# Routing weights spread from SBUF instead of DRAM, and the two ends of an expert stage put in another order

## The reference, cut to what matters

```
scores   = sigmoid(x @ gate_w.T)                    # 32 experts
# best 2 of 4 groups, then the best 8 experts of a token;
# their scores, normalised and times 2.5, are its weights, all others are 0
out      = sum over e of weight[t, e] * down_e(silu(gate_e(x)) * up_e(x))   # 32 routed experts
out     += the shared expert of inner width 256     # no weight; done as 2 units of 128
# second layer: attention, then a feed-forward whose weights w1, w2 are rounded to
# integers after division by a scale = max|w| / 127
```

## Time and profile before

| | us |
|---|---|
| median of 3 runs (417.43 to 422.83) | 417.8 |
| the profiled execution, its own time | 418.78 |
| span of its trace | 417.0 |
| PE busy | 386.8 (93%) |
| DVE busy | 258.8 (62%) |
| ACT busy | 187.5 (45%) |
| POOL busy | 131.3 (31%) |

### The profile page before, as it was taken

One profiled execution on the slowest core, in us unless ns is written; L12 is line 12 of the kernel. 1 busy time (PEld: TensorE's weight loads), 2 busy tenths in 40 slices (PEclk: granted clock), 3 DMA queues, 4 the chain that ended last, 5 costly groups with the idle time before them and its releaser, 6 DMA issues.

```text
span 417.0 us, 8560 instructions
## 1 busy us (share of the span) xinstructions
PE 386.8 (93%) x3269; PEld 314.5 (75%) x3269; DVE 258.8 (62%) x525; ACT 187.5 (45%) x401; POOL 131.3 (31%) x109
## 2 busy tenths in 40 slices
PE   8898699998999899999999999999988999999675
PEld 6554478656787687999999999999986755567333
DVE  0258877589876854555555555555564558844686
ACT  0154722348342533444444554444435488634171
POOL 0125300163030052344333334433385047620012
PEclk9999989998999999999999999999999999999798
DMA  8940000300042006254554554444200000000001
GB/s 300 331 173 2 3 3 2 101 0 4 2 163 66 0 9 230 68 137 134 135 145 145 155 142 147 134 134 146 84 0 0 2 0 2 2 3 1 0 2 58
DMA packets 13916, 32.96 MB, mean 79 GB/s; under 512 B 1760, under 2 KB 3744, under 8 KB 13376
## 3 DMA queue, kind: packets, MB, share of 16 engines
q1 hardware_dynamic: 12000, 30.66, 23.4%
q10 hardware_dynamic: 1888, 1.91, 1.3%
HBM read 31.88 MB, written 0.68 MB: 78 GB/s over the span
## 4 chain that ended last, share of the span: by engine, by line
PE 69%; DVE 19%; ACT 5%; issue 4%; DMA 2%; ACTq 1%; POOL 0%; DVEq 0%
PE psum L1087 68%; DVE rc L847 3%; DMA region<-in_w_lin 2%; DVE rn L826 1%; ACT region L725 1%; DVE xn L774 1%; DVE nt L768 1%; DVE rn L825 1%; DVE nt L770 1%; DVE nt L771 1%; DVE region L848 1%; DVE xc L759 1%; DVE ra L816 1%; ACT sq L541 1%; DVE al L985 1%
## 5 line engine op out<-in xcount | busy, mean ns | idle before, releaser
L1087 PE MATMUL psum<-xh,split_all 128*128 128x296 f32 x544 | 122.9, 300 | 1.4 <-DVE rt L927 1.3
L443 POOL TENSOR_TENSOR split_all<-km,split_all 128x768 fp32r<-128x768 f32 x34 | 63.3, 1863 | 115.9 <-ACT split_all L654 115.9
L1087 PEld LDWEIGHTS psum<-xh,split_all 128*128 128x128 f32 x544 | 91.7, 188 | 2.7 <-DVE rt L927 1.8
L1087 PE MATMUL psum<-xl,split_all 128*128 128x296 f32 (+1 forms) x288 | 85.1, 300 | 0.0
L1087 PE MATMUL psum<-ah,split_all 128*128 128x296 f32 x272 | 67.6, 302 | 2.6 <-DVE al L985 2.0
L674 ACT ACTIVATE ah<-rt 128x296 fp32r<-128x296 f32 x68 | 30.7, 452 | 80.6 <-DVE rt L983 74.3
L1087 PEld LDWEIGHTS psum<-xl,split_all 128*128 128x128 f32 (+1 forms) x288 | 53.2, 187 | 3.2 <-issue 2.8
L985 DVE TENSOR_TENSOR al<-rt,ah 128x296 fp32r<-128x296 f32 x64 | 31.9, 498 | 33.1 <-ACT ah L674 33.1
L1087 PEld LDWEIGHTS psum<-ah,split_all 128*128 128x128 f32 x272 | 47.8, 189 | 5.0 <-DVE al L985 2.5
L980 DVE TENSOR_TENSOR rb<-psum,wb 128x296 f32<-128x296 f32 x60 | 28.0, 467 | 26.4 <-ACT psum L672 26.4
L1087 PE MATMUL psum<-al,split_all 128*128 128x296 f32 x136 | 40.8, 300 | 0.0
(11 more groups left out here) (179 smaller groups left out, 579.0 us busy)
## 6 DMA issues: line engine op xcount, KB each, us to landing
km<-in_experts SPq DMA_DIRECT2D x34, 384.0 KB, 4.0
wb<-weights SPq DMA_DIRECT2D x30, 296.0 KB, 3.7
w_sb<-in_w SPq DMA_DIRECT2D x2, 1024.0 KB, 11.9
region<-in_x SPq DMA_DIRECT2D x6, 296.0 KB, 5.5
region<-in_g_wo SPq DMA_DIRECT2D x1, 1024.0 KB, 4.9
region<-in_l_wo SPq DMA_DIRECT2D x1, 1024.0 KB, 5.0
region<-in_w_lin ACTq DMA_DIRECT2D x6, 128.0 KB, 6.7
qkv_sb<-in_qkv_w SPq DMA_DIRECT2D x1, 768.0 KB, 6.0
```

Source lines behind the costliest of these rows:

```text
L443: nc.gpsimd.tensor_tensor(wl[i], ring[i], wh[i].bitcast(f32), ALU.subtract)\
L1087: return nc.tensor.matmul(out_, lhsT, rhs, start=start, stop=stop, skip_group_check=True)
```

## The change

- The scratch tensor in DRAM, its store and the two selections by PE are gone. Each of the 32 routed units gets its row by a DMA whose source is the row's one partition of `wrow`, read once for each of the 128 partitions it is written to. SP's loop is written out.
- Head: all four first high parts are made before the normalisation, and POOL makes the four low parts in one go; the scale of w1 and w2 is worked out before the router; the sigmoid table is loaded before the tokens are rounded; the shared units use banks 4, 5 and 6, 7 in turn.
- `down_sums` issues its four matmuls on `ah` first and waits for `al` only before the last two.
- Tail: w1 and w2 are quantised and region is cleared in small pieces, one behind each low part from unit 4 on.

```
-BUSY = ((7, (0, 4, 14)), (0, (5, 0, 10)), (3, (5, 4, 8)), (7, (6, 4, 14)), (3, (5, 4, 10)))
+BUSY = ((7, (0, 4, 14)), (0, (5, 0, 10)), (3, (5, 0, 8)), (7, (6, 4, 14)), (3, (5, 4, 10)))
+WPIECES, VPIECES = 8, 8
+VZ = 1 + VPIECES + 2
...
-            def spread_weights(i, row):
-                sp.dma_start(wb[:, i, :], row.broadcast_to([P, T])).then_inc(s_wb[i], 16)
+            def spread_weights(u):
+                row = wrow[u - SHARED:u - SHARED + 1, :].unsqueeze(1).broadcast_to([1, P, T])
+                sp.dma_start(wb[:, u % NRING, :], row).then_inc(s_wb[u % NRING], 16)
 
             for u in range(NRING, 2 * NRING):
-                if u == NRING + 2:
-                    sp.wait_ge(s_wrow, 2)
-                    sp.dma_start(weights, wrow[:, 0:T]).then_inc(s_wout, 16)
-                    sp.wait_ge(s_wout, 16)
-                    for i in range(NRING):
-                        spread_weights(i, weights[NRING + i - SHARED:NRING + i - SHARED + 1, :])
                 load_expert(u, experts[u, :, :])
...
+            sp.wait_ge(s_wrow, 2)
+            for u in range(SHARED, NRING + SHARED):
+                spread_weights(u)
+            for u in range(2 * NRING, UNITS + SHARED):
+                if u < UNITS:
+                    load_expert(u, experts[u, :, :])
+                sp.wait_ge(s_act, 2 * (u - SHARED + 1 - NRING))
+                spread_weights(u - SHARED)
...
+            for u in range(NRING, UNITS):
                 low_part(u, u % NRING)
...
+                k = u - NRING
+                if k == 0:
+                    pool.wait_ge(s_sc, 1)
+                    pool.wait_ge(s_wo, 4)
+                if k < 2 * WPIECES:
+                    quantise_piece(k)
+                elif k < 2 * WPIECES + VPIECES:
+                    clear_piece(k - 2 * WPIECES)
...
-            for i in range(AHEAD):
+            for i in range(NRING):
                 high_part(i, i, 0, False)
             norm(2)
+            load_table(ACT.Sigmoid)
...
             centre(2)
+            reduce_peaks(0, 2, 6, 1)
             norm_apply(2, 6)
...
-            reduce_peaks(0, 2, 7, 1)
+            scales_of(0, 2, 7, 1).then_inc(s_sc, 1)
...
             for u in range(SHARED, NRING):
+                dve.wait_ge(s_wb[u], 16)
                 for j in range(2):
-                    dve.wait_ge(s_sel, 2 * (u - SHARED) + j + 1)
-                    expert_unit(2 * u + j, j, sg[:, j, :], ps[6 + j][:, 0:HALF])
+                    expert_unit(2 * u + j, j, ps[6 + j][:, 0:HALF], wb[:, u, half(j)])
...
+                pe.wait_ge(s_ah, n + 1)
+                for m in range(C):
+                    cols = slice(2 * D + m * P, 2 * D + (m + 1) * P)
+                    for w in (wh, wl):
+                        mm(ps[2 * m + hf][:, 0:HALF], w[i][:, cols], ah[:, hf, :], False, False)
                 if shared:
                     pe.wait_ge(s_alp, n + 1)
                 else:
                     pe.wait_ge(s_al, n + (1 - 2 * SHARED))
                 for m in range(C):
                     cols = slice(2 * D + m * P, 2 * D + (m + 1) * P)
-                    ins = three(ps[2 * m + hf][:, 0:HALF], (wh[i][:, cols], wl[i][:, cols]),
-                                (ah[:, hf, :], al[:, hf, :]), False, False)
+                    ins = mm(ps[2 * m + hf][:, 0:HALF], wh[i][:, cols], al[:, hf, :], False, False)
```

More of the change, by code:

```diff
@@ L165, in program @@
         zeros = sb("zeros", [P, HALF], bf16)
[L166 removed]
+        wrow = sb("wrow", [EXPERTS, T])
         xh = sb("xh", [P, C, T], f32r)
@@ L475, in _, with quantise_piece @@
[L475 to L478, removed]
+            for i in range(NRING):
+                low_part(i, i)
+            for n in range(2 * SHARED):
+                activation_low_part(n, n % 2)
+            def quantise_piece(k):
+                w, wq_ = ((w1_sb, w1q), (w2_sb, w2q))[k // WPIECES]
+                cols = slice(k % WPIECES * WPIECE, (k % WPIECES + 1) * WPIECE)
+                nc.gpsimd.tensor_scalar(w[:, cols], w[:, cols], inv[:, k // WPIECES:k // WPIECES + 1], ROUND,
+                                        ALU.mult, ALU.add).then_inc(s_wqt, 1)
+                pool.wait_ge(s_wqt, k + 1)
+                nc.gpsimd.tensor_scalar(wq_[:].rearrange("p c n -> p (c n)")[:, cols], w[:, cols], 1.0, -ROUND,
+                                        ALU.mult, ALU.add).then_inc(s_wq, 1)
@@ new lines, in clear_piece @@
+            def clear_piece(k):
+                cols = slice(k * VPIECE, (k + 1) * VPIECE)
+                nc.gpsimd.memset(region[:, cols], 0.0).then_inc(s_vz, 1)
+            for u in range(NRING, UNITS):
+                low_part(u, u % NRING)
+                k = u - NRING
[6 more added lines that the diff above has]
+                    clear_piece(k - 2 * WPIECES)
+                elif k == 2 * WPIECES + VPIECES:
+                    pool.wait_ge(s_vz, 1 + VPIECES)
+                    pool.wait_ge(s_wsl, u + 1)
+                    for b in range(2):
+                        nc.gpsimd.memset(v16[64 * b:64 * b + S, :, :, b, HD:HD + 1], 1.0).then_inc(s_vz, 1)
+                    pool.wait_ge(s_vz, VZ)
@@ L667, in _, with expert_unit @@
             load_table(ACT.Silu)
-            def expert_unit(n, j, gate):
+            def expert_unit(n, j, gate, bank=4):
                 act_e.wait_ge(s_g, n + 1)
-                nc.scalar.activation(gate, ps[4][:, 0:HALF], ACT.Silu).then_inc(s_sg, 1)
+                nc.scalar.activation(gate, ps[bank][:, 0:HALF], ACT.Silu).then_inc(s_sg, 1)
                 act_e.wait_ge(s_act, n + 1)
                 nc.scalar.activation(ah[:, j, :], act[:, j, :], ACT.Copy).then_inc(s_ah, 1)
[L676 to L679, removed]
+            for i in range(SHARED):
+                for j in range(2):
+                    expert_unit(2 * i + j, j, sg[:, j, :], 4 + 2 * j)
+            for i in range(SHARED, NRING):
+                if i == SHARED:
+                    act_e.wait_ge(s_wrow, 2)
+                expert_unit(2 * i, 0, ps[6][:, 0:HALF])
+                high_part(i + AHEAD, (i + AHEAD) % NRING, (i + AHEAD) // NRING)
+                expert_unit(2 * i + 1, 1, ps[7][:, 0:HALF])
             with act_e.Fori(1, (UNITS - AHEAD) // NRING) as r:
@@ L1369, in three, with up_sums @@
                 return mm(out_, w_lo, x_hi, False, stop)
-            def up_sums(u, i, hf, first=False):
-                n = 2 * u + hf
+            def up_sums(u, i, hf, bank=4, waits=None):
+                n = 2 * u + hf if waits is None else waits
                 if hf == 0:
                     pe.wait_ge(s_wsl, u + 1)
-                if not first:
+                if waits != 0:
                     pe.wait_ge(s_sg, n)
@@ L1379, in up_sums @@
                     cols = slice(c * INNER, (c + 1) * INNER)
-                    ins = three(ps[4][:, 0:HALF], (wh[i][:, cols], wl[i][:, cols]),
+                    ins = three(ps[bank][:, 0:HALF], (wh[i][:, cols], wl[i][:, cols]),
                                 (xh[:, c, half(hf)], xl[:, c, half(hf)]), c == 0, c == C - 1)
                 ins.then_inc(s_g, 1)
-                if not first:
+                if waits != 0:
                     pe.wait_ge(s_act, n)
@@ L1642 @@
     out = nc.dram_tensor("out", (P, C, T), mybir.dt.float32, kind="ExternalOutput").ap()
-    weights = nc.dram_tensor("weights", (EXPERTS, T), mybir.dt.float32, kind="Internal").ap()
-    program(nc, *args, weights, out)
+    program(nc, *args, out)
     r = run_bass_kernel_spmd(nc, [{f"in_{k}": arrays[k] for k in _ORDER}], core_ids=[0])
```

91 lines of the change are left out of this document (24 added, 67 removed).

## The result

| | before | changed |
|---|---|---|
| median | 417.62 (416.55 to 422.83, 4 runs) | **605.52** (605.06 to 607.14, 4 runs) |
| ratio to before | 1 | 1.4519 [1.4475, 1.4563] |
| profiled execution: its time, its span | 418.78, 417.0 | 607.14, 605.3 |
| PE busy | 386.8 (93%) | 442.7 (73%) |

One of the four executions before, 422.83, is 1.5% above the fastest of the same kernel; the ratio goes without it.

What follows compares the result with a forecast made beforehand. Rows of weights read from one SBUF partition, not PE, were to bound the expert stage: 153.4 + 1.7 + 364.8 = 519.9, plus 7.0 to the stage's end and 98.7 after gives span 625.6, time 627 us; range 412 to 660.

Steps and rivals of the forecast that it cites:

- rival A: Expert stage: rows from SBUF as fast as from DRAM, only the two ends change; 414 us, chance 0.31.
- A row, 11.4 us: Expert stage: 303,104 bytes from one SBUF partition at one engine's 26.6 GB/s, 11.4 us for each of 32 rows.
- First row, 1.7 + 11.4 = 13.1: Start of the expert stage: 1.7 us fixed landing time, then 11.4 us for the first row.
- Head, 1.7 earlier: Up to the first row's issue: table load, scale instructions and POOL's low parts moved, so `wrow` is ready 1.7 us earlier.
- Tail, 7.0: Last row's first product to stage end: 5.5 before, 0.5 less by the split, 2 more by a lower clock; 7.0 us.
- The rest, 98.7: After the expert stage, from 318.3 to 417.0 before: untouched by the change, 98.7 us.
- The expert loads, 0 or 24: 26 expert loads in the same queue as the rows: counted as 0, or 24 us more if they come on top.
- a landing of 30 us or more: DMA row wb<-wrow: median of 30 us or more from issue to landing, because three rows wait in front.
- The other signs: Expert stage: DMA engines busy at 0.8 and over while moving under 70 GB/s; clock row with digits under 9.
- Rival B: Rows of weights: one partition can feed two engines' streams, 5.7 us a row; 443 us, up to 467; chance 0.10.
- rival C: Rows of weights: worse than one stream, time lost between pieces; 10% on the row gives 663 us; chance beyond 660 0.05.
- POOL's pieces, 0.27 each and a fixed part: POOL in the expert stage: quantising w1 and w2 in eighths, 0.27 us each plus a fixed part, hidden by the rows' wait.

Runs made afterwards that it cites:

- the DMA kernel: A kernel of DMAs alone, nothing of the model, each kind three times and waited for; one SBUF partition to 128 took 12.62 us, a DRAM row 3.37.
- The version with the selections: The changed kernel with the DRAM scratch back as source of the rows, and units 2 and 3 by PE's selection as before; 412.75 us, ratio 0.9908.

## Why the prediction was right, and where its terms were off

The place, the wait and the sign were right: one source partition gives the 16 engines together 27 GB/s, each unit waits for its row, and 627 was 3.6% over 605.5. The range of 412 to 660 alone would say little, as it takes in rival A; what bears the account is that the terms came out one by one. One step was lucky: I took 26.6 GB/s as one engine's share of the best window and reasoned from the engine to the partition. The runs show a limit of a group of four partitions, which 3.2 busy engines nearly reach as 12 do; that it comes so near to an engine's share is not explained by any run. Term by term:

- **A row, 11.4 us: 10.83.** This is the mis-sized term, 31 x 0.57 = 17.7 of the 20.3 us between the two spans. I took 26.6 GB/s from the best window; the same group gives 27.0 (11.2 us), and at every fourth row, ahead of a change of group, 1 to 2 us are saved. The Trainium skill, in SBUF — State Buffer, section Door 1: The DMA port swizzle, has the nearer figure, 27.2 GB/s for a port and 11.1 us by my estimate from it (11.14 unrounded, so 8 us less in the sum and not 9); 13.60 against 4.77 us agrees with its port of four neighbours here. The intervals at a change of port are neither in its figures nor in mine.
- **First row, 1.7 + 11.4 = 13.1: 13.38** from the issue at 152.06 to the product at 165.44.
- **Head, 1.7 earlier:** `wrow` was copied by 152.03 instead of 155.07. Of the 3.0 us, 0.9 is that this execution came to the router earlier (`xn` at 135.92, before at 136.85); 2.1 is the order. The other traces bear this out: `xn` stands anywhere from 135.5 to 137.2 with either head, and from there to the last copy of `wrow` it is 18.2 us in each of the three executions with the old head and 16.0 to 16.1 in each with the new. The two last steps of the router, 1.03 and 0.83 in the earlier trace rows, now take 0.32 each, 1.2 us less in all where I took 0.9; that fits POOL's work beside them as what had held them, though no run changes that alone.
- **Tail, 7.0: 5.4,** from 501.14 to 506.5. The clock did fall to its lower level, but only for the last piece, where I had it for all. The first two lines are windows (PE's busy time first, the granted clock third from last), the others PE's timeline:

```profile
501.00:503.00 2.00, 0.77 (x5) 0.77 (x6) 1.24 (x3) 0.76 (x2) 0.00 (x0) 1.00 0.00 0
503.00:506.50 3.50, 3.49 (x15) 2.93 (x13) 1.46 (x4) 0.45 (x1) 0.00 (x0) 0.53 0.00 0
...
503.15 1.16 PE L1090 MATMUL psum<-ah,split_all 128*128 128x296 f32 x4
...
505.79 0.69 PE L1090 MATMUL psum<-al,split_all 128*128 128x296 f32 x2
```

  The twelve last matmuls take 3.35 us, from 503.15 to 506.5, where twelve at 0.136 are 1.63. So the clock took 1.7, near my 2; what I overrated is the rest, 3.7 in place of 5.0. PE had done all but the last six of its matmuls on `xh` and `xl` while it waited for the row, which fits.

- **The rest, 98.7: 98.75,** from 506.55 to 605.3. **The expert loads, 0 or 24: 0.** A row on the same group with a load beside it takes 11.2 us in the kernel, and 303,104 bytes at the 27.0 GB/s of the DMA kernel, with no load, are 11.2 as well.
- **What I expected to see and did not:** a landing of 30 us or more. I had three rows waiting in front of each; SP is held at the issue with about two on the way, which no row of the profile before could show, because none of its DMAs is slow. It cost nothing here, since the stream never ran dry. The other signs came: DMA at 0.8 and over with 25 to 84 GB/s, and digits of 7 and 8 among the 9s of the clock row.
- **Rival A** has its head and its tail borne out, not its whole sum. It summed to 4.6 us gained (414 against the 418.8 of the execution): 0.7 of head left after the wait for the first row, 2.1 for the selections, 1.8 of tail. The version with the selections has neither that wait nor the 2.1, so of rival A's terms it has 1.7 + 1.8 = 3.5; it gained 3.9, and 4.5 by the end of the stage (313.73 in place of the earlier trace rows's 318.27). That this is near 4.6 is chance. The version nearest to rival A, all rows from DRAM and no selections, gained 1.6. PE waited 3.99 us for its first row: my sum had the wait take back "most of" 1.7, but there the row starts after a store, 1.7 us more, which rival A with its rows from SBUF did not need. Rival A itself can't be had, since no row from SBUF is fast. **Rival B,** two streams, is excluded by 27.0 GB/s; **rival C** by 605.5.
- **POOL's pieces, 0.27 each and a fixed part:** 0.76 and 0.41. The pair takes 1.16, not 0.8, and still fits in the 4.90 of a unit beside a low part of 1.84.

## What to carry to other kernels

Price a broadcast by the source side as well: bytes read from one group of four SBUF partitions, divided by the 27 GB/s measured here, against the time the pipeline has for it. A round trip through DRAM looks like waste and was 3.4 us against 12.6, with 1.7 us for the store once. When the chain names a load, look at what stands in front of it in the queue before mending the load.

## What the runs showed of the hardware that I had not expected

- SP's issue of a DMA is held while about two slow ones are on the way: 20.51 us for four issues, 8.6 to 11.1 us for most later ones, against 1.76 for four fast ones. With every fourth row slow, one of them and the expert load behind it were enough to hold the next issue for 4.6 to 4.8 us.
- Two rows from different groups of four, from one queue or two, take 21.5 to 21.8 us; from the same group 23.8. Four engines at partitions 0 to 3 move the same bytes in 13.60 us, so a quarter of the engines would nearly do for a row (12.62), but it is spread over up to 16.
- DMA share is no measure of bytes: alone in its kernel, the single-partition DMA keeps the engines 0.76 busy at 24 GB/s.

- Small pieces on POOL cost more than their share of columns: 256 columns took 0.76 us where 2048 took 2.13, so eight pieces take 6.0.
